# A cross-attention and quantised-FFN block on one core: K projected in plain fp32, the opening's conversions and waits put in another order, q in two buffers

## The reference

```python
def _L0_xattn_ref(q, k, v, Wq, Wo):          # k = v = ctx_1024
    Q = _split(q @ Wq.T, N_HEADS)
    K = _split(k @ Wq.T, N_HEADS)
    V = _split(v @ Wq.T, N_HEADS)            # the same numbers as K
    scores = jnp.einsum('bhqd,bhkd->bhqk', Q, K) / jnp.sqrt(jnp.asarray(d_k, Q.dtype))
    attn = jax.nn.softmax(scores, axis=-1)
    out = jnp.einsum('bhqk,bhkd->bhqd', attn, V)
    return out.transpose(0, 2, 1, 3).reshape(b, s, h * dk) @ Wo.T

def _L0_ffn_ref(x, clip_x, clip_down, w_gate, w_up, w_down):
    xq = _act_fake_quant(x, clip_x[0])
    gate = jnp.einsum('bsh,ih->bsi', xq, _weight_fake_quant(w_gate))
    up = jnp.einsum('bsh,ih->bsi', xq, _weight_fake_quant(w_up))
    h = _act_fake_quant(jax.nn.silu(gate) * up, clip_down[0])
    return jnp.einsum('bsi,hi->bsh', h, _weight_fake_quant(w_down))

x = x + _L0_xattn_ref(_layernorm(x), ctx_1024, ctx_1024, L0_xattn_Wq, L0_xattn_Wo)
x = x + _L0_ffn_ref(_layernorm(x), ...)
```

## Time and profile before

| what | value |
|---|---|
| median of 3 runs | 1109.43 us (1109.39 to 1111.11) |
| the profiled execution | 1110.75 us, span 1109.0 us |
| PE busy | 1086.8 us, 98% of the span |
| DVE busy | 793.9 us, 72% |
| ACT busy | 624.8 us, 56% |
| POOL busy | 392.5 us, 35% |
| mean granted TensorE clock | 0.997 of full speed |

### The profile page before, as it was taken

How to read it: one execution, slowest core, us unless ns; L and a number is a source line. 1 busy time by engine, 2 the same in 40 slices (tenths; PEclk the granted TensorE clock), 3 DMA queues, 4 the chain that set the end, 5 groups by cost and what they waited for, 6 DMA issues and landing times. The chain is left out here.

```text
span 1109.0 us, 17280 instructions
## 1 busy us (share of the span) xinstructions
PE 1086.8 (98%) x6181; PEld 614.3 (55%) x6181; DVE 793.9 (72%) x1419; ACT 624.8 (56%) x768; POOL 392.5 (35%) x317
## 2 busy tenths in 40 slices
...
GB/s 255 122 105 125 200 178 158 172 195 178 161 148 180 152 157 148 179 143 103 70 64 248 173 146 254 218 246 217 249 218 162 70 64 95 285 415 428 427 398 227
DMA packets 121605, 214.35 MB, mean 193 GB/s; under 512 B 59056, under 2 KB 68144, under 8 KB 110384
## 3 DMA queue, kind: packets, MB, share of 16 engines
...
...
## 5 line engine op out<-in xcount | busy, mean ns | idle before, releaser
L474 POOL TENSOR_TENSOR a_aT<-a_att,a_aT 128x512 fp32r<-128x512 f32 x64 | 83.5, 1305 | 297.5 <-ACT a_aT L547 297.5
L849 PE MATMUL a_Q<-a_xT,wq 128*128 128x512 f32 x732 | 186.1, 403 | 1.3 <-DVE wq L623 1.3
L1010 ACT ACTIVATE e_sg<-e_G,x_gus 128x512 f32<-128x512 f32 x176 | 119.3, 686 | 114.3 <-PE e_G L1122 114.3
L1238 POOL TENSOR_TENSOR x<-x,c_y 128x512 f32<-128x512 f32 x32 | 55.0, 1752 | 363.0 <-DVE c_y L1282 343.3
L1082 DVE SCALAR_TENSOR_TENSOR h<-e_U,x_gus,e_sg 128x512 f32<-128x512 f32 x176 | 131.9, 750 | 69.8 <-PE e_U L1126 44.4
L1126 PE MATMUL e_U<-e_cT,gu 128*128 128x512 bf16 x704 | 180.7, 379 | 0.0
L1122 PE MATMUL e_G<-e_cT,gu 128*128 128x512 bf16 x704 | 180.7, 379 | 0.0
L811 PE MATMUL a_O<-a_wo,a_aT 128*128 128x512 f32 x720 | 175.2, 392 | 0.0
L849 PEld LDWEIGHTS a_Q<-a_xT,wq 128*128 128x128 f32 x732 | 134.1, 190 | 51.6 <-issue 23.9
L811 PEld LDWEIGHTS a_O<-a_wo,a_aT 128*128 128x128 f32 x720 | 132.2, 188 | 27.8 <-issue 2.9
L544 ACT ACTIVATE a_pr<-a_S 77x2048 f32<-77x2048 f32 x64 | 120.2, 1878 | 37.5 <-PE a_S L834 37.5
...
## 6 DMA issues: line engine op xcount, KB each, us to landing
...
a_xt<-in_xT SPq DMA_DIRECT2D x64, 256.0 KB, 4.0
a_xr<-in_x SPq DMA_DIRECT2D x64, 256.0 KB, 3.3
x_d<-a_xr SPq DMA_DIRECT2D x64, 256.0 KB, 2.6
a_xs<-in_x SPq DMA_DIRECT2D x60, 256.0 KB, 3.8
...
```

Source lines behind the costliest of these rows:

```text
L849: mm = nc.tensor.matmul(q_bank(n.n)[:], wq[:, wp, j, P * n.g:P * (n.g + 1)], xT[:, n.par, xp, j], start=(ins == 0), stop=(ins == 3 * KT - 1))
L1010: nc.scalar.activation(sg[:, s], G[:, t % GU], ACT.Silu, scale=gus[:, t:t + 1]).then_inc(silued, 1)
```

## The change

- K is projected by 16 plain fp32 matmuls from the loaded tiles wq32 and cx32. The splits of both, on ACT, DVE and POOL, are gone, and the sums over Wq's rows stand among the projections.
- On DVE the low part of the centred Wq comes behind the statistics of block 0, in slot -5. Before it stood ahead of them.
- On ACT `root(0)` stands behind the third xT copy, ahead of the fourth and of all work of slot -5. Before it stood at the end of that slot.
- `turn_rs(0)` stands ahead of item 0's projection on PE; the copies to `rsb` of blocks 0 and 1 go from DVE to ACT (`copy_factors`).
- The low part of K goes from DVE (slots -6 and -5) to POOL (slot -1). The maxima no longer wait for it, the scores do.
- q32 has two buffers; DVE's scaling waits for POOL's low part of the item before the last.
- The banks of q's first items are Q and O in turn; `maxima_at` is gone, each item's maxima stand in slot n - 3; V's four transposes and copies stand one to a slot, in slots -2 to 1.
- Two small DVE instructions on the clips go from slot -2 to slot 5.
- SP's list of transfers is the same in both kernels.

Core of the diff (declarations of semaphores are left out, and the margin is narrower than in the file):

```diff
     wq32 = tmp("p_wq32", [P, KT, D])
-    wr = tmp("p_wr", [P, 2, KT, D], F32R)
     cx32 = tmp("p_cx32", [P, KT, NK])
-    cx = tmp("p_cx", [P, 2, KT, NK], F32R)
+    k32 = tmp("p_k32", [P, GROUPS, NK])
 aT = sb("a_aT", [P, 2, 2, KT, TOK], F32R)
...
 kt = sb("a_kt", [P, BATCH, 2, GROUPS, KEYS], F32R)
-k32 = sb("a_k32", [P, GROUPS, NK])
 kbd = sb("a_kbd", [P, 2, GROUPS, HG, KEYS], F32R)
...
 att = sb("a_att", [P, TOK])
-q32 = sb("a_q32", [P, TOK])
+q32 = sb("a_q32", [P, 2, TOK])
 rsb = sb("a_rsb", [P, 2, TOK])
...
 def q_bank(n):
-    return (Q, O, DN)[n] if n < 3 else O if n == 4 else Q
-Q_FREE = (0, 0, 0, 1, 2, 4)
-def maxima_at(k):
-    return {-3: (), -2: (0,), -1: (1, 2)}.get(k, (k + 3,))
+    return O if n in (1, 3, 5) else Q
+Q_FREE = (0, 0, 1, 2, 3, 4, 5)
 def projection(n):
 def v_bank(b):
-    return (A, DN)[b % 2]
+    return A if b == 0 else DN
 with nc.Block() as block:
...
         nc.gpsimd.memset(epsb[:], EPS).then_inc(consts, 1)
-        pool.wait_ge(cx_in, 16)
-        pool.wait_ge(p_hi, 2)
-        nc.gpsimd.tensor_tensor(cx[:, 1].rearrange("p k n -> p (k n)"), cx32[:].rearrange("p k n -> p (k n)"),
-                                cx[:, 0].rearrange("p k n -> p (k n)").bitcast(F32), ALU.subtract).then_inc(cx_lo, 1)
         def spread_k(b, j):
...
                 pool.wait_ge(qT_h, n.n + 1)
-                nc.gpsimd.tensor_tensor(qT[:, n.ring, 1], q32[:], qT[:, n.ring, 0].bitcast(F32), ALU.subtract).then_inc(qT_l, 1)
+                nc.gpsimd.tensor_tensor(qT[:, n.ring, 1], q32[:, n.n % 2], qT[:, n.ring, 0].bitcast(F32), ALU.subtract).then_inc(qT_l, 1)
+            if k == -1:
+                pool.wait_ge(k32_rdy, 1)
+                for g in range(GROUPS):
+                    nc.gpsimd.tensor_tensor(kt[:, :, 1, g], k32[:, g].rearrange("p (b k) -> p b k", b=BATCH),
+                                            kt[:, :, 0, g].bitcast(F32), ALU.subtract).then_inc(k_lo, 1)
             if k == -5:
...
         nc.scalar.preload_act_table_set("natural_log_exp_and_others")
-        def split_wq(n):
-            act.wait_ge(wq_in[n], 16)
-            nc.scalar.activation(wr[:, 0, 2 * n:2 * n + 2], wq32[:, 2 * n:2 * n + 2], ACT.Copy).then_inc(p_hi, 1)
...
             nc.scalar.activation(r0[:], lnv[:], ACT.Exp, scale=-0.5).then_inc(r0_rdy, 1)
+        def copy_factors(b):
+            act.wait_ge(r_turned, b + 1)
+            nc.scalar.activation(rsb[:, b], A[:], ACT.Copy).then_inc(rsb_rdy, 1)
         def copy_v(b):
...
             nc.scalar.activation(v[:, b], v_bank(b)[0:KEYS], ACT.Copy).then_inc(v_rdy, 1)
-        split_wq(0)
-        act.wait_ge(cx_in, 16)
-        nc.scalar.activation(cx[:, 0], cx32[:], ACT.Copy).then_inc(p_hi, 1)
-        split_wq(1)
         for k in SLOTS:
...
             for n in measured_at(k):
-                if n.g == TT - 1 and n.block > 0:
+                if n.g == TT - 1:
+                    if n.block == 0:
+                        act.wait_ge(consts, 2)
                     root(n.block)
...
                     nc.scalar.activation(kt[:, :, 0, g], S[:, g, 0:NK].rearrange("p (b k) -> p b k", b=BATCH), ACT.Copy).then_inc(k_hi, 1)
+                copy_factors(0)
                 nc.scalar.activation(k32[:], S[:, :, 0:NK], ACT.Copy).then_inc(k32_rdy, 1)
-                act.wait_ge(consts, 2)
-                root(0)
                 act.wait_ge(clip_in, 32)
                 nc.scalar.activation(esig[:], clips[:], ACT.Exp, scale=-1.0).then_inc(esig_rdy, 1)
+            if k == 0:
+                copy_factors(1)
             if (n := at(k, 4)):
...
                 act.wait_ge(q_scaled, n.n + 1)
-                nc.scalar.activation(qT[:, n.ring, 0], q32[:], ACT.Copy).then_inc(qT_h, 1)
-            if k == -1:
-                for b in range(BATCH):
-                    copy_v(b)
+                nc.scalar.activation(qT[:, n.ring, 0], q32[:, n.n % 2], ACT.Copy).then_inc(qT_h, 1)
+            if -2 <= k < BATCH - 2:
+                copy_v(k + 2)
             if k == STEPS + 3:
...
         own = Chain(dve, own_d)
-        for n in range(2):
-            dve.wait_ge(p_hi, 2 * n + 1)
-            nc.vector.tensor_tensor(wr[:, 1, 2 * n:2 * n + 2], wq32[:, 2 * n:2 * n + 2], wr[:, 0, 2 * n:2 * n + 2].bitcast(F32),
-                                    ALU.subtract).then_inc(p_lo, 1)
         def measure(w):
...
                                                    op0=ALU.mult, op1=ALU.add).then_inc(centred, 1)
+            if k == -5:
                 for n in range(2):
...
                                             wq[:, 0, 2 * n:2 * n + 2].bitcast(F32), ALU.subtract).then_inc(wc_lo, 1)
-            if k in (-6, -5):
-                for g in (0, 1) if k == -6 else (2, 3):
-                    dve.wait_ge(k_hi, g + 1)
-                    dve.wait_ge(k32_rdy, 1)
-                    nc.vector.tensor_tensor(kt[:, :, 1, g], k32[:, g].rearrange("p (b k) -> p b k", b=BATCH),
-                                            kt[:, :, 0, g].bitcast(F32), ALU.subtract).then_inc(k_lo, 1)
-            if k == -5:
-                dve.wait_ge(r_turned, 1)
-                nc.vector.tensor_copy(rsb[:, 0], A[:]).then_inc(rsb_rdy, 1)
-                dve.wait_ge(rsb_rdy, 1)
-            if k == -2:
+            if k == 5:
                 dve.wait_ge(esig_rdy, 1)
...
             if (n := at(k, 4)):
-                if n.n == TT:
-                    dve.wait_ge(r_turned, 2)
-                    nc.vector.tensor_copy(rsb[:, 1], A[:]).then_inc(rsb_rdy, 1)
-                    dve.wait_ge(rsb_rdy, 2)
                 dve.wait_ge(q_done, n.n + 1)
-                after(dve, qT_l, n.n)
+                after(dve, qT_l, n.n - 1)
+                if n.n in (0, TT):
+                    dve.wait_ge(rsb_rdy, n.block + 1)
                 if n.block > 1:
                     dve.wait_ge(rsb_in[n.par], 16 * (n.block // 2))
-                nc.vector.tensor_tensor(q32[:], q_bank(n.n)[:], rsb[:, n.par], ALU.mult).then_inc(q_scaled, 1)
-            for n in (Item(m) for m in maxima_at(k) if 0 <= m < STEPS):
+                nc.vector.tensor_tensor(q32[:, n.n % 2], q_bank(n.n)[:], rsb[:, n.par], ALU.mult).then_inc(q_scaled, 1)
+            if (n := at(k, 3)):
                 dve.wait_ge(m_scored, n.n + 1)
...
             nc.tensor.matmul(Q[:, 0:P], allones[:], allones[:], start=True, stop=True)
-        for j in range(KT):
-            if j % 2 == 0:
-                pe.wait_ge(wq_in[j // 2], 16)
+        def sum_w(j):
             mm = nc.tensor.matmul(A[:], allones[:], wq32[:, j], start=(j == 0), stop=(j == KT - 1))
-        mm.then_inc(wsum, 1)
-        for n, (wp, cp) in enumerate(((0, 0), (0, 1), (1, 0))):
-            if n == 1:
-                pe.wait_ge(cx_lo, 1)
-            for g in range(GROUPS):
-                for j in range(KT):
-                    if g == 0 and j % 2 == 0 and n != 1:
-                        if n == 0:
-                            pe.wait_ge(p_hi, 2 + j // 2)
-                        else:
-                            pe.wait_ge(p_lo, 1 + j // 2)
-                    mm = nc.tensor.matmul(S[:, g, 0:NK], wr[:, wp, j, P * g:P * (g + 1)], cx[:, cp, j],
-                                          start=(n + j == 0), stop=(n == 2 and j == KT - 1))
-                if n == 2:
-                    mm.then_inc(k_done, 1)
+            if j == KT - 1:
+                mm.then_inc(wsum, 1)
+        def project_k(g, j):
+            mm = nc.tensor.matmul(S[:, g, 0:NK], wq32[:, j, P * g:P * (g + 1)], cx32[:, j], start=(j == 0), stop=(j == KT - 1))
+            if j == KT - 1:
+                mm.then_inc(k_done, 1)
+        pe.wait_ge(wq_in[0], 16)
+        sum_w(0)
+        sum_w(1)
+        pe.wait_ge(cx_in, 16)
+        for g in range(GROUPS // 2):
+            project_k(g, 0)
+        pe.wait_ge(wq_in[1], 16)
+        sum_w(2)
+        sum_w(3)
+        for g in range(GROUPS):
+            for j in range(KT):
+                if j > 0 or g >= GROUPS // 2:
+                    project_k(g, j)
         def project_v(b):
-            if b % 2 == 0:
+            if b == 0:
                 pe.wait_ge(rsb_rdy, 1)
-            else:
-                pe.wait_ge(q_scaled, 3)
             pe.wait_ge(k32_rdy, 1)
-            after(pe, v_rdy, b - 1)
+            after(pe, v_rdy, b if b > 1 else 0)
             for g in range(GROUPS):
...
             if b == 1:
-                pe.wait_ge(v_rdy, BATCH)
+                pe.wait_ge(v_rdy, 1)
             for t in range(TT):
...
                     pe.wait_ge(kbd_rdy, HG * (n.batch + 1))
-                    pe.wait_ge(k_lo, GROUPS)
+                    pe.wait_ge(k32_rdy, 1)
                 pe.wait_ge(qT_h, n.n + 1)
...
                 mm.then_inc(scored, 1)
+            if k == -4:
+                turn_rs(0)
             if (n := at(k, 4)):
...
                 mm.then_inc(q_done, 1)
-            if k == -3:
-                turn_rs(0)
             if k == 0:
...
             if at(k, 4):
-                for m in maxima_at(k):
```

(13 more changed lines are left out.)

2 lines of the change are left out of this document (1 added, 1 removed).

## The result

The median went from 1110.03 us (1109.39 to 1111.11, 4 runs) to 1103.41 us (1102.53 to 1104.49, 4 runs): a ratio of 0.9939, 95% interval 0.9924 to 0.9955. The forecast was 1099.8. The profiled execution took 1103.94 us, its span is 1102.1 against 1109.0: 6.9 us less.

What follows compares the result with a forecast made beforehand. PE was taken to bound the kernel, so an earlier steady pace counts: 6.9 us of start plus 2.8 of clock, 9.7 off 1110.75, gives 1101.1; with the median 1.3 lower, 1099.8 us. Range 1097.5 to 1105.5.

Steps and rivals of the forecast that it cites:

- the first rival: Clock falls all the same in PE's gap before item 0's scores; only 6.9 us come, 1102.5 us; chance 0.2.
- the chain: Summed durations of the opening, sums and K to item 0's scores: first q scaling at 23.3 us, scores at 44.4.
- Then PE has no gap: PE from 23.2 us: q, maxima and transposes, 19.4 us of work without idling, to 42.6.
- stands where DVE has no instruction of that kind to block: K's low part on POOL, slot -1: no DVE instruction there contends for the shared port; 2.8 to 4.8 us, hidden.
- the loop through one buffer: Opening before: q goes round DVE, ACT and POOL once per item, 2.81 us; item 1's scaling waits 1.33 for POOL.
- The order of maxima and V: PE's opening from 23.2 us: five maxima at 0.65 us and four V transposes at about 0.4, within 19.4 us.
- The order of root and Wq's low part: Opening on ACT and DVE: root to 16.7 us, Wq's low part to 21.3, item 0 scaled at 23.3, not 27.55.
- The clock: At the gap before item 0's scores, now 1.8 us instead of 2.67, the clock holds: 2.8 us more gained.
- The price of a fall: Between the starts of item 0's and item 1's scores: 9.27 us against 6.48, the 2.79 us being the clock.
- the sum: Whole kernel: 6.9 us of earlier start plus 2.8 of clock, 9.7; the median 1.3 below the profiled execution.

Runs made afterwards that it cites:

- e1: Changed kernel plus one wait: POOL starts K's low parts only when DVE has finished the factors of block 1; 1100.44 us.
- e2: Changed kernel with q32 in one buffer again, DVE waiting for POOL's low part of the item just before; 1103.13 us.
- e12: e1 with q32 in one buffer again; 1103.31 us.
- e6: Kernel before with only the two q buffers and DVE's wait moved back by one item; 1107.32 us.
- e10: e1 with the old order of the first maxima and of V, with its banks; 1104.01 us.
- e3: Changed kernel with K projected the old way, by splits and 48 matmuls; 1105.25 us.
- e5: Kernel before with only K's projection changed to plain fp32 matmuls, without the splits; 1108.62 us.
- e7: e1 with the old places of DVE's low part of Wq, root(0) and the first factor transpose; 1101.86 us.

## Why the prediction was right, and what it missed

The direction, the place (all of it ahead of PE's steady pace) and the main part, the earlier start of item 0's scores, were right: 5.66 us of the 6.9 forecast came. The time lies in the stated range, but not where the forecast put it: no execution of the changed kernel came below 1102.03 us, and the medians, 1103.4 and 1103.6, lie nearer the first rival's 1102.5 than the forecast's 1099.8.

- K's 14 plain matmuls took 7.42 us, 0.53 each instead of 0.60, and ended at 17.3 instead of 18.8. PE then waited 1.24 us for the factors of block 0, whose last instruction was held up by POOL (17.15), so this gave nothing. DVE's low part of Wq came behind the same instruction. No run takes this blocking away, so its price is open.
- Centring at 10.17 (10.4), the high part of Wq on ACT done at 18.9 (19.5), its low part at 20.91 (21.3), first scaling at 23.11 (23.3): the chain held within 0.6 us. The two low parts took 2.59 us together, 1.3 each: POOL's reads blocked them less than I allowed.
- "Then PE has no gap" is the step that failed, and in it the sentence that K's low part on POOL "stands where DVE has no instruction of that kind to block". It has four, the factors of block 1, 128x4 each. I had counted DVE's scalings, maxima and statistics in slot -1 and left out these, since they are 0.8 us. They took 3.0 (2.1 of it beside K's low part, the first 0.79 beside q's), PE idled 1.46 us, and the scores started at 45.68 instead of 44.4. e1 takes the blocking away and gets 1.6 us back. The row at 36.39 us, with one tensor input, waits like the three with two. The Trainium skill ("SBUF — State Buffer", section "Who interferes with whom") says that a DVE instruction with two SBUF inputs contends with a GpSimd one that reads SBUF, that tensor_scalar can contend too, in a two-port mode, and that the loser blocks for the whole instruction; the four rows agree, 0.70 to 0.79 us against 0.16 to 0.17. I applied the rule to the large instructions only.
- The reason for the old delay was named as the loop through one buffer. That is part of it: 1.0 us (e2 and e12) to 1.8 (e6). The order of maxima and V, which the prediction put into the chain but gave no price of its own, is worth 1.9 us of start (e10), the plain K 2.4 (e3, more than half of it clock) to 3.0 (e5). The order of root and Wq's low part, which it made the backbone of the new opening, is worth nothing in the start of the scores (e7): q of item 0 is early in either. These prices were taken in different surroundings and don't add up to the 5.66 us.
- The clock: I took it to hold. It held in 4 of 9 executions of the changed kernel (1102.03 to 1102.89 us); in the others the time was 1103.59 to 1104.49, 1.5 us more. The first rival, a fallen clock, had a chance of 0.2; it came in five of nine. The price of a fall was taken as 2.8 us from one trace. In the changed kernel it is 1.6 (8.04 us from item 0's scores to item 1's, against 6.44 undisturbed). Besides, the sum took off 1.3 us more for the distance between the profiled execution and the median. Over all runs the kernel before took 1109.2 to 1109.7 us at a mean clock of 0.998 and 1110.2 to 1111.4 at 0.995, so this distance is mostly clock as well, and was counted twice; with a held clock the chain gives 1101.1, not 1099.8.
- The sum: of 9.7 us, 6.9 came in the profiled execution; 1.3 are the late start, for which the factors of block 1 are enough (1.6 in e1), and 1.6 the clock. At clock 1.000 the kernel before took 1107.6 to 1107.9 and the changed one 1102.0 to 1102.9: 4.7 to 5.9 us, which takes in the measured gain of start, 5.66.
- Behind 60 us nothing was given back, as predicted, and K's low part on POOL ended at 38.56, 7 us ahead of its use.

Open: why the clock falls in one gap and not in another of the same length. That was not settled. In the traces it fell at gaps of 1.81 us (after, e7) to 3.79 us (e3), and didn't at others of 1.84 (e12), 2.23 (e7) and 2.70 us (e6 and the kernel before); with one gap filled it still fell, at an earlier one.
